# Attention of all nodes on all (layer 1) as three products of rounded parts, in a four-layer graph attention network on one core

## What is computed

```python
out = relu(x @ mlp1_w + mlp1_b)                    # 512 nodes x 512
# _gat(out, None, W_fc, a_fc): every node attends to every node, there is no mask
h = inp @ W                                        # 512 x 512
f1, f2 = h @ a[:F_], h @ a[F_:]
e = leaky_relu(f1[:, :, None] + f2[:, None, :], 0.2)
att = softmax(e, axis=2)
h_prime = elu(att @ h)
out = elu(h_prime) + residual
out = relu(out @ mlp2_w + mlp2_b)                  # 512 x 256
out = _gat(out, adj, W_hand, a_hand)               # and so on
```

## Time and profile before

| | |
|---|---|
| median of three runs | 3206.72 us |
| the profiled execution's own time | 3213.97 us |
| its span, first to last instruction | 3212.2 us |
| mean granted TensorE clock | 0.99 |
| TensorE matmuls busy | 3128.8 us, 97% of the span |
| VectorE busy | 2638.4 us, 82% |
| ScalarE busy | 1865.3 us, 58% |
| GpSimd busy | 333.8 us, 10% |
| 16 DMA engines | 13 GB/s, under 5% |

### The profile page before, as it was taken

The page is one execution under the profiler, slowest core; times in us unless marked ns, Lnnn a source line. Parts: engine busy times, 40 slices in busy tenths (PEclk is TensorE's granted clock), DMA queues, the critical chain, the costliest instruction groups (busy, mean ns, idle before and its releaser), DMA issues.

```text
span 3212.2 us, 55473 instructions
## 1 busy us (share of the span) xinstructions
PE 3128.8 (97%) x20480; PEld 2857.5 (89%) x20480; DVE 2638.4 (82%) x7557; ACT 1865.3 (58%) x4639; POOL 333.8 (10%) x281
## 2 busy tenths in 40 slices
PE   8999999999999999999999999999999999999997
PEld 7898898999898998898988999988989988898885
DVE  5788888888888888888888888888888888887866
ACT  2655656565565556565556565555555655555564
POOL 1201111011111011111011110011110111110110
PEclk7999999999999999999999999999999999999999
DMA  2000000000000000000000000000000000000000
GB/s 73 8 1 14 14 14 14 14 1 14 14 14 14 7 8 14 14 14 14 1 14 14 14 14 14 1 14 14 14 14 12 3 14 14 14 14 1 1 1 27
DMA packets 16316, 41.32 MB, mean 13 GB/s; under 512 B 5296, under 2 KB 6832, under 8 KB 16048
## 3 DMA queue, kind: packets, MB, share of 16 engines
q1 hardware_dynamic: 16048, 37.77, 3.4%
HBM read 20.99 MB, written 16.78 MB: 12 GB/s over the span
## 4 chain that ended last, share of the span: by engine, by line
PE 81%; DVE 12%; ACT 3%; POOL 2%; issue 2%; SPq 0%; DMA 0%; POOLq 0%; ACTq 0%; DVEq 0%
PE bank L502 28%; PE bank L560 14%; PE bank L593 14%; PE bank L631 14%; PE bank L548 3%; PE bank L516 3%; POOL oTlo L1166 2%; DVE R L767 2%; PE bank L643 2%; DVE Z L729 1%; DVE Z L970 1%; DVE Z L902 1%; DVE x L973 1%; PE bank L538 1%; DVE x L919 1%
## 5 line engine op out<-in xcount | busy, mean ns | idle before, releaser
L560 PE MATMUL bank<-hw,R 128*128 128x257 f32 x3072 | 729.5, 381 | 6.3 <-ACT Z L1118 2.8
L560 PEld LDWEIGHTS bank<-hw,R 128*128 128x128 f32 x3072 | 561.6, 189 | 98.6 <-issue 14.2
L593 PEld LDWEIGHTS bank<-hw,R 128*128 128x128 f32 x4096 | 509.5, 196 | 10.6 <-issue 1.0
L593 PE MATMUL bank<-hw,R 128*128 128x65 f32 x4096 | 507.7, 275 | 0.6 <-DVE R L767 0.6
L631 PE MATMUL bank<-hw,R 128*128 128x257 f32 (+1 forms) x2048 | 499.2, 382 | 0.0
L767 DVE SCALAR_TENSOR_TENSOR R<-bank,E,mask_ne 128x512 f32<-128x512 f32 x640 | 459.0, 740 | 11.9 <-PE bank L548 5.5
L631 PEld LDWEIGHTS bank<-hw,R 128*128 128x128 f32 x2048 | 372.5, 189 | 46.0
L1159 POOL TENSOR_TENSOR rs<-ve,mhalf 128x4 f32<-128x4 f32 x128 | 141.6, 1106 | 2554.7 <-DVE ve L708 2554.7
L502 PE MATMUL bank<-wfc_hi,oThi 128*128 128x256 f32 (+1 forms) x1024 | 304.0, 297 | 32.0 <-POOL oTlo L1166 28.3
L1001 ACT COPY Z<-bank 128x258 f32<-128x258 f32 (+1 forms) x640 | 235.2, 373 | 138.3 <-PE bank L502 132.6
L502 PE MATMUL bank<-wfc_lo,oThi 128*128 128x256 f32 (+1 forms) x1024 | 288.8, 282 | 0.0
(11 more groups left out here) (211 smaller groups left out, 6812.3 us busy)
## 6 DMA issues: line engine op xcount, KB each, us to landing
x<-in_x_dram SPq DMA_DIRECT2D x32, 512.0 KB, 3.3
out_dram<-x SPq DMA_DIRECT2D x32, 512.0 KB, 2.6
R<-in_adj_dram SPq DMA_DIRECT2D x2, 512.0 KB, 6.9
Z<-in_L_gnn_mlp_w_dram SPq DMA_DIRECT2D x2, 512.0 KB, 5.6
hw<-in_L_gnn_W_fc_dram SPq DMA_DIRECT2D x1, 1024.0 KB, 8.1
R<-in_L_gnn_W_dram SPq DMA_DIRECT2D x1, 256.0 KB, 3.8
R<-in_L_gnn_W_hand_dram SPq DMA_DIRECT2D x1, 256.0 KB, 7.0
rowt<-in_L_gnn_W_dram SPq DMA_DIRECT2D x1, 256.0 KB, 4.9
```

The costliest lines, as they stand in the source:

```text
L560: ins = e.matmul(bk[:, 0:257], P[:, j, i * 128:(i + 1) * 128], hw[:, j, 0:257], start=(j == 0), stop=(j == NBLK - 1))
L593: ins = e.matmul(bk[:, i * 66:i * 66 + 65], P[:, (4 * h + j) % PTILES, i * 128:(i + 1) * 128], hv[:, j, h, 0:65], start=(j == 0 and i == 0 ...
```

## The change

What is done differently in layer 1:

- VectorE's tiles P take in the sender's weight: `E[:, 2]` times the row, and the maximum with `E[:, 1]`, which now is the exponential with other constants (`kshift2`, scale 1). So h is no longer multiplied by the weight, and `hw` isn't written in layer 1 (`scale(1)` and the scaling of `hs2` are gone). The denominator comes from a column of ones beside h (column 256 of `HA["hi"]`, written once at the start; column 257 is zero).
- h is split: ScalarE copies the banks of `h1` and `hs2` to `HA["hi"]` and `HB["hi"]` (fp32r), VectorE subtracts these from the banks into `HA["lo"]` and `HB["lo"]` (`low_part`, 8 new instructions of 128 x 256 per batch). A bank is free after the latter. `HB` lies in the lane's `hT`. ScalarE's copy to `raw` shrinks to the 2 score columns.
- P is split: ScalarE copies each tile to `oT["hi"]` (4 new instructions of 128 x 512 per batch, `Phi`), GpSimd writes `oT["lo"]` (4 new ones, `Plo`).
- `attf` uses `mm3`: three fp32r products of 258 or 256 columns for one fp32 product of 257 or 256.
- Moved with it: the copies of `r3` go to `rowt` and `R[s][:, 4]` instead of `hw`, `Sb` has a tile of its own, the weights of `WFC` are staged in `O1` at the start.
- All strings in `TURNS` are new.

```diff
@@ tensor_batch
             for q in range(8):
-                i, c0, n = q // 2, q % 2 * 257, 257 - q % 2
+                i, H, n = q // 2, (HA, HB[s])[q % 2], 258 - q % 2 * 2
+                cols = slice(i * 128, (i + 1) * 128)
                 w.wait_ge(*freed(b, "attf", q))
                 for j in range(NBLK):
-                    w.wait_ge(*at("P", b, 4, j))
-                    w.wait_ge(*at(("hw", "hw2")[q % 2], b, *((0, j) if q % 2 == 0 else (j,))))
-                    ins = e.matmul(bank_of(b, "attf", q)[:, 0:n], P[:, j, i * 128:(i + 1) * 128],
-                                   hw[:, j, c0:c0 + n], start=(j == 0), stop=(j == NBLK - 1))
+                    w.wait_ge(*at("Plo", b, j))
+                    w.wait_ge(*at(("hAlo", "hBlo")[q % 2], b, j))
+                    ins = mm3(e, bank_of(b, "attf", q)[:, 0:n], (oT["hi"][:, j, cols], oT["lo"][:, j, cols]),
+                              (H["hi"][:, j, 0:n], H["lo"][:, j, 0:n]), j == 0, j == NBLK - 1)
@@ vector_batch
+            def low_part(kind, name):
+                H = HA if kind == "hA" else HB[s]
+                for n in range(NBLK):
+                    w.wait_ge(*at(kind, b, n))
+                    e.tensor_tensor(H["lo"][:, n, 0:F], bank_of(b, name, n)[:, 0:F], f32(H["hi"][:, n, 0:F]),
+                                    ALU.subtract).then_inc(up(kind + "lo", b))
+                    yield
...
             yield from normalize(1)
+            yield from low_part("hA", "h1")
             yield from scores(1, 1)
+            yield from low_part("hB", "hs2")
             w.wait_ge(*at("E", b, 1, 1))
             w.wait_ge(*at("rowc", b, 0))
+            w.wait_ge(*at("E", b, 1, 2))
             for j in range(NBLK):
-                e.tensor_scalar(P[:, j, :], rowt[s][:, 0:512], m["E"][:, 1, 0, j:j + 1], None, ALU.max).then_inc(up("P", b))
+                e.tensor_scalar(P[:, j, :], rowt[s][:, 0:512], m["E"][:, 2, 0, j:j + 1], m["E"][:, 1, 0, j:j + 1],
+                                ALU.mult, ALU.max).then_inc(up("P", b))
@@ scalar_batch
-            yield from evacuate(1, 258)
-            yield from exps(1, 1, 0.2, wcol)
+            for n in range(NBLK):
+                w.wait_ge(*at("h", b, 1, n))
+                e.copy(raw[s][:, n, 256:258], bank_of(b, "h1", n)[:, 256:258]).then_inc(up("raw", b))
+                e.copy(HA["hi"][:, n, 0:F], bank_of(b, "h1", n)[:, 0:F]).then_inc(up("hA", b))
+                yield
+            yield from exps(1, 1, 0.2, m["E"][:, 2, 0:1, :])
...
-            yield from scale(1)
             for n in range(NBLK):
                 w.wait_ge(*at("hs2", b, n))
-                e.activation(hw[:, n, 257:513], bank_of(b, "hs2", n)[:, 0:256], ACT.Copy,
-                             scale=hw[:, n, 256:257]).then_inc(up("hw2", b))
+                e.copy(HB[s]["hi"][:, n, :], bank_of(b, "hs2", n)[:, 0:F]).then_inc(up("hB", b))
+                yield
+            for j in range(NBLK):
+                w.wait_ge(*at("P", b, 4, j))
+                e.copy(oT["hi"][:, j, :], R[s][:, j, :]).then_inc(up("Phi", b))
                 yield
@@ pool_batch
+            for j in range(NBLK):
+                w.wait_ge(*at("Phi", b, j))
+                e.tensor_tensor(oT["lo"][:, j, :], R[b % LANES][:, j, :], f32(oT["hi"][:, j, :]),
+                                ALU.subtract).then_inc(up("Plo", b))
+                yield
@@ TURNS, the cycle of TensorE (112 steps in both)
-        ("2211211110011110011122002202212112111201212110221212011010012020100220212102011001121100200110112111"
-         "222121221111"),
+        ("2200112111100001101221002212211200121102222212121111111011101210200021122121211112000001121111100100"
+         "122222221111"),
```

More of the change, by code:

```diff
@@ L33 @@
     "rowc": (1,), "hw0": (4,), "att0": (4, 4), "den0": (4, 2), "y0": (4,), "e0": (4, 2), "x0": (4, 2),
[1 row of a table removed]
+    "m1": (4,), "m1a": (4,), "o1hi": (4,), "o1lo": (4,), "hs2": (4,), "hA": (4,), "hAlo": (4,), "hB": (4,), "hBlo": (4,),
+    "Phi": (4,), "Plo": (4,), "attf": (8,), "rDf": (4,),
     "ef": (8, 2), "mf": (8,), "ef2": (8,), "zf": (8,), "zT": (4,), "o2": (4,), "o2hi": (4,), "o2lo": (4,),
@@ L47 @@
     + [("hT1", k, "hTlo", (1, k)) for k in range(2)] + [("m1", i, "m1a", (i,)) for i in range(4)]
-    + [("h1", i, "raw", (1, i)) for i in range(4)]
-    + [("TM1", 0, "sc", (1, 1)), ("hs2", 0, "hw2", (0,)), ("row", 4, "rowc", (0,))]
-    + [("hs2", i, "hw2", (i,)) for i in range(1, 4)]
+    + [("h1", i, "hAlo", (i,)) for i in range(4)]
+    + [("TM1", 0, "sc", (1, 1)), ("hs2", 0, "hBlo", (0,)), ("row", 4, "rowc", (0,))]
+    + [("hs2", i, "hBlo", (i,)) for i in range(1, 4)]
     + [("attf", q, "ef", (q, 1)) for q in range(8)] + [("zT", k, "o2", (k,)) for k in range(4)]
@@ L117 @@
         ("21"),
-        ("05441312230"),
+        ("12544331020"),
     ),
@@ L1006, in exps @@
                 w.wait_ge(s_const, 1)
-                if l == 0 and b == 2:
-                    w.wait_ge(s_wlo, K_BEFORE[3] - 2)
-                    w.wait_ge(s_wT, 5)
-                for out, src, sc in ((m["E"][:, 0, 0:nh, :], 1, -(1.0 - alpha)), (m["E"][:, 1, 0:nh, :], 0, 1.0 - alpha),
-                                     (last, 0, alpha)):
-                    e.activation(out, m["A"][:, src, 0:nh, :], ACT.Exp, bias=kshift[:, 0:1], scale=sc).then_inc(up("E", b))
+                second = (1.0, kshift2) if l == 1 else (1.0 - alpha, kshift)
+                for out, src, sc, shift in ((m["E"][:, 0, 0:nh, :], 1, -(1.0 - alpha), kshift),
+                                            (m["E"][:, 1, 0:nh, :], 0, *second), (last, 0, alpha, kshift)):
+                    e.activation(out, m["A"][:, src, 0:nh, :], ACT.Exp, bias=shift[:, 0:1], scale=sc).then_inc(up("E", b))
                 yield
@@ L1208, in _ @@
             w.wait_ge(s_const, 1)
+            for p, q, v in (("hi", F, -2.0), ("hi", F + 1, 0.0), ("lo", F, 0.0), ("lo", F + 1, 0.0)):
+                e.tensor_scalar(HA[p][:, :, q], mhalf[:, :], v, None, ALU.mult)
             e.tensor_copy(identr[:, :], id_st).then_inc(s_id)
```

100 lines of the change are left out of this document (54 added, 46 removed), and 3 rows, old and new, of tables (ONCE, SHARED).

## The result

| | before | after |
|---|---|---|
| median of the runs made side by side | 3210.67 us (5 runs) | 3193.93 us (5 runs) |
| ratio to before, 95% interval | | 0.9948 [0.9934, 0.9961] |
| the profiled execution's own time, span | 3213.97, 3212.2 us | 3197.34, 3195.5 us |
| mean granted TensorE clock | 0.99 | 0.983 |

The change makes the kernel 17 us faster. The forecast was 3115 us (3080 to 3180), a gain of 92 us; the time lies outside the range.

A forecast was written before the change was run, and what follows sets the result against it. The prediction took TensorE's instruction stream as the bound. From the profiled 3214 us it summed -77 (products), -41 (oTlo wait), +16 (hs2 to attf) and +8 (end) to 3120, 3115 for the median of runs; range 3080 to 3180.

The forecast's parts named there:

- Products, -77: In attf, three fp32r products replace one fp32 product, saving 0.075 us each over 1024 products: 77 us.
- Changes between fp32 and fp32r, 0: On TensorE, 592 places where fp32r follows fp32, before 472, cost nothing together; 10 us if only half counted.
- The wait for oTlo goes, -41: Between m1 and h1, 24 products cover TensorE's wait for GpSimd's oTlo: 1.4 us a batch, 41 us saved.
- What stands between hs2 and attf, +16: The new five-hop chain to Plo is barely covered ahead of attf; 0.5 us a batch of new waiting, 16 us.
- VectorE, slack and not time: VectorE's added low parts, 3.4 us, and Plo's hold, 3.0 us a batch, raise its load to 88.3 us, costing slack only.
- ScalarE, 0: ScalarE's copies changed in layer 1 add net 0.8 us a batch; busy 58 of 97 us, so no time.
- End, +8: In the last batches no other lane covers the chain to attf: 5 to 8 us once or twice, 8 in the sum.
- Rival 2: New chain late: GpSimd holds VectorE, TensorE waits 2 us a batch or keeps oTlo's wait; about 3160 us, chance 0.23.

The follow-up runs named there:

- fp32_attf: The changed kernel with each attf product as one fp32 product of P with rounded h instead of three fp32r ones: 3267.2 us, ratio 1.0181 to before.
- before_hi_h1: The kernel before, with h1's third product reading oThi so h1 doesn't wait for oTlo, which GpSimd still writes: 3220.3 us, ratio 1.0028 to before.
- before_no_otlo: The kernel before without GpSimd's four oTlo a batch; h1 and hs2 read oThi in the third product: 3159.7 us, ratio 0.9847 to before.
- no_otlo: m1_first without GpSimd's four oTlo a batch; h1 and hs2 read oThi in the third product: 3157.9 us, ratio 0.9842 to before.
- no_plo: The changed kernel without GpSimd's four Plo a batch; attf's third product reads the rounded P: 3171.5 us, ratio 0.9874 to before.
- no_gps: m1_first without GpSimd's oTlo and Plo, so GpSimd has no work in layer 1: 3139.8 us, ratio 0.9784 to before.
- no_gps_no_low: no_gps also without VectorE's eight low parts of h a batch: 3137.6 us, ratio 0.9762 to before.
- no_low: The changed kernel without VectorE's eight low parts of h a batch; attf's second product reads rounded h again: 3177.6 us, ratio 0.9901 to before.
- m1_first: The changed kernel with ScalarE's last block of m1 moved ahead of three steps in its cycle, an Exp among them: 3192.0 us, ratio 0.9937 to before.
- otlo_dve: m1_first with the oTlo of batches 2 to 26 written by VectorE, right behind ScalarE's block, instead of GpSimd: 3251.0 us, ratio 1.0130 to before.

## Why the prediction was wrong, point by point

- **Products, -77.** Right: 73 by fp32_attf, 2.41 us a batch by the starts. The Trainium skill's four passes for an fp32 product ("FP8 and Floating Point Precision", TensorE Precision Notes), which would have made it 121, don't fit this kernel: fp32_attf has the difference of 0.433 and 0.358.
- **Changes between fp32 and fp32r, 0.** Right within what shows: what is left is 1.05 against 0.95 us a batch, 3 us in all.
- **The wait for oTlo goes, -41.** This step failed: the waits did not fall by 1.4 us a batch but rose from 1.67 to 2.83, 0.9 of them for oTlo. It took 3.4 us from m1's last product to GpSimd's last end out of the trace of before and put 24 products in the place, as if the other engines' times stood fixed. But those 3.4 us were made by the hold and by ScalarE's order, and in after ScalarE's last block of m1 stands behind a step that waits for VectorE. The text had the hold at that very place in its rows and costed only the hold that was new. before_hi_h1 shows that the wait was worth nothing by itself, before_no_otlo that the hold behind it was worth 50 us of before's time.
- **What stands between hs2 and attf, +16.** Too much: TensorE waits for Plo 0.8 us once in the whole run. With 0.1 to 0.5 us of reckoned slack it was covered. That TensorE comes later by its other waits may be the reason, but isn't shown: no_otlo, with 0.9 us a batch fewer of these, doesn't wait for Plo in the 1000 us either.
- **VectorE, slack and not time.** Half right. The load is 0.890 x 96.5 = 85.9 us (forecast 88.3); the Plo hold is 1.4 us in the two groups named, with P's own last tile some 2.0 (by the windows of after and no_plo, 890.3 and 875.3 in 1000), not 3.0. "P stays one instruction of 479 ns" didn't hold: with two numbers per sender it takes 538, and 1.5 us where it meets the first Plo, which the prediction had said under its second rival and left out of this step. The low parts cost nothing by themselves. But Plo's hold costs 18 to 22 us of time, which the step denied, and the low parts cost 16 when it is there: VectorE is ahead of TensorE only until it gets to m1.
- **ScalarE, 0.** Right for its load, wrong for its order: 1.45 us a batch in no_gps are waits for banks that it reads late; in before_no_otlo there are 0.34. That is 1.1 us a batch, some 35 us, and no term of the sum had it.
- **End, +8.** Start and end gave back 24. In no_gps they are 856.7 us, 24 less than in after, and from before_hi_h1 to before_no_otlo they fall by 22 as well: most of it goes with GpSimd's passes. Whether VectorE's hold or TensorE's own wait for oTlo costs more there, isn't shown.

The distance from 3120 to the profiled 3197 is made up so: waits +28 in place of -41 + 16, that is 53; half clock and rest 8; start and end +24 in place of +8, that is 16.

Rival 2 named half of it ("or keeps the wait for oTlo") and priced it at 41; with the banks and the ends it costs 80. Its own mechanism, TensorE late at Plo, didn't come, though P was held as it said. no_gps_no_low, where nothing of the new work of GpSimd and VectorE is left, is still 22 us above the forecast: its waits are 1.6 us a batch, all for ScalarE's banks, where the sum had 1.67 - 1.4 + 0.5 = 0.8. The other 0.8, the period of 94.94 against 94.1, covers that.

## What to carry to other kernels

A wait in a trace is the last link of a chain: before its length is put into a sum, follow the engine that was late back to what held it, and ask whether that holds something else a microsecond later. Read an engine's load in the stretch where it is waited for, not over the cycle; in the kernel before 84% in the mean was 97% there, in the one after the two were alike. And a step moved to another engine should stand in that engine's order where its input is already there: one and the same edit was 57 us slower or 20 us faster by one to three places.

## What the runs showed of the hardware

- Hold of VectorE by GpSimd: a 128x256 instruction of VectorE with two inputs in SBUF grows from 0.42 to 0.48 us up to 1.52 beside a 1.4 us pass of GpSimd, as the earlier trace rows had it. A tensor_scalar with one input tile in SBUF is held too: P, 128x512, takes up to 1.51 us beside Plo and at most 0.55 in no_plo. The Trainium skill ("SBUF — State Buffer", Who interferes with whom) states this exclusion, and the trace agrees. That 4 passes a batch could cost 50 us of 3210 I had not expected.
- Half clock after a wait: in after the granted clock fell in four places of the cycle, each time within 2 us of TensorE's wait of 1.8 us for line 1020. The stretch right after the one at 1031.10 (eighth number: clock), and the next:

```profile
1031.70:1035.10 3.40, 3.40 (x18) 3.40 (x17) 2.05 (x6) 0.56 (x4) 1.53 (x2) 0.50 0.02 5
1035.10:1038.50 3.40, 3.40 (x31) 3.40 (x30) 3.03 (x10) 0.78 (x6) 0.00 (x0) 1.00 0.01 2
```

  18 products in place of 31 in 3.4 us at half of full speed, 1.2 GHz. Of the waits of some 1.8 us or more for a bank of ScalarE in the cycle, 4 of 8 in after were followed by this, 6 of 9 in before_hi_h1, and 6, 2 and 1 of 8 in fp32_attf, no_plo and no_low; of the 17 waits of 1.2 us for oTlo in after none was, and m1_first, with no wait over 1.3 us in the cycle, has no such stretch there. In otlo_dve, where waits come in pairs 2 us apart (1.4 and 1.5 us in two lanes, 0.4 and 1.4 in the third), there are 17. What decides between two waits of the same length stays open.
